# Fused preln layer: half of the first x loads, and the four writes of the second normalised rows, issued by ScalarE instead of SyncE

## The reference

```python
def ternary_quantize(w):
    delta = 0.7 * jnp.mean(jnp.abs(w))
    return jnp.where(w > delta, 1.0, jnp.where(w < -delta, -1.0, 0.0))

x = x + dynconv(_layernorm(x), w_lin)     # softmax taps, 31 wide, causal, 16 heads of 64
x = x + einsum("bsd,od->bso", _layernorm(x), ternary_quantize(weight) * alpha) + bias
```

## Time and profile before

| | us |
|---|---|
| runs shown | 418.83 and 427.5, median 423.17 |
| profiled execution | 418.44 |
| its span, on core 4, the slowest | 416.9 |
| spans of the eight cores | 404.3 to 416.9 |
| PE / DVE / ACT busy on core 4 | 161.0 / 132.6 / 71.0 |

### The profile page before, as it was taken

How to read it: one execution, slowest core, us unless ns; L and a number is a source line. 1 busy time by engine, 2 the same in 40 slices (tenths; PEclk the granted TensorE clock), 3 DMA queues, 4 the chain that set the end, 5 groups by cost and what they waited for, 6 DMA issues and landing times.

```text
span 416.9 us, 2975 instructions; the slowest of 8 cores (404.3 to 416.9 us)
## 1 busy us (share of the span) xinstructions
PE 161.0 (39%) x934; PEld 92.4 (22%) x940; DVE 132.6 (32%) x250; ACT 71.0 (17%) x78; POOL 5.8 (1%) x8
## 2 busy tenths in 40 slices
PE   0000030420300070016006769169430099999690
PEld 0000000100000030002002669169430033343230
DVE  1222592258220031103302297527360013232221
ACT  0000346751211023103201100000005341200000
POOL 5000000000000000000000000000000000000000
PEclk9999985855555577559556855555555579999896
DMA  7999824000499954974461599999403756999422
GB/s 179 288 300 282 283 108 100 0 1 0 101 179 224 253 101 102 234 141 99 150 158 25 119 199 241 222 182 232 74 0 112 108 142 149 259 274 241 128 101 101
DMA packets 85544, 64.53 MB, mean 155 GB/s; under 512 B 69008, under 2 KB 70032, under 8 KB 85528
## 3 DMA queue, kind: packets, MB, share of 16 engines
q10 hardware_dynamic: 13072, 37.82, 32.3%
q1 hardware_dynamic: 71352, 25.50, 31.3%
q0 software_dynamic: 1104, 1.02, 1.7%
HBM read 23.14 MB, written 25.40 MB: 116 GB/s over the span
## 4 chain that ended last, share of the span: by engine, by line
DMA 35%; SPq 27%; DVE 11%; PE 10%; ACT 7%; issue 4%; DVEq 3%; ACTq 2%
SPq L224 10%; DMA xs<-x 9%; SPq L207 9%; SPq L199 8%; DMA stage<-wpad 6%; DMA xn2d<-xn2r 6%; DMA xn1d<-xn 5%; DMA wet<-stage 4%; PE ps_at L617 3%; PE ps_wp L590 3%; DMA xn1T<-xn1d 3%; ACT wet L447 2%; ACT wet L446 2%; DVE redt L313 2%; DVE statsw L137 2%
## 5 line engine op out<-in xcount | busy, mean ns | idle before, releaser
L590 PE MATMUL ps_wp<-wlTb,xn1T 128*128 128x496 bf16 x128 | 37.4, 462 | 128.3 <-DMA xn1T<-xn1d 105.1
L617 PE MATMUL ps_at<-wins,wet 128*64 128x64 bf16 x512 | 50.8, 305 | 24.5 <-DMA wet<-stage 18.0
L617 PEld LDWEIGHTS ps_at<-wins,wet 128*64 128x64 bf16 x512 | 50.2, 216 | 25.4 <-issue 25.4
L590 PEld LDWEIGHTS ps_wp<-wlTb,xn1T 128*128 128x128 bf16 x128 | 14.3, 115 | 151.0 <-issue 142.8
L347 DVE TENSOR_REDUCE sumc<-wpad 128x16 f32<-128x496 bf16 x16 | 10.7, 669 | 110.7 <-ACT wpad L463 110.5
L642 PE MATMUL ps_ff<-wtern,xn2T 128*128 128x512 bf16 x64 | 26.7, 417 | 28.4 <-DMA xn2T<-xn2d 28.1
L137 DVE BATCH_NORM_STATS2 statsw<-xs 128x6 f32<-128x512 f32 x32 | 22.0, 688 | 31.4 <-DMA xs<-x 30.0
L554 ACT ACTIVATE xn2r<-xs,scn,scr 128x1024 bf16<-128x1024 f32 x16 | 18.5, 1228 | 52.9 <-DVEq L380 26.5
L357 DVE TENSOR_TENSOR xs<-ps_at,xs 128x1024 f32<-128x1024 f32 x16 | 19.6, 1223 | 23.7 <-PE ps_at L617 23.7
L640 PE MATMUL ps_ff<-wtern,xn2T 128*128 128x512 bf16 x60 | 25.1, 418 | 3.3 <-DMA xn2T<-xn2d 3.3
L463 ACT ACTIVATE wpad<-ps_wp,cstb 128x496 bf16<-128x496 f32 x16 | 10.6, 671 | 86.0 <-PE ps_wp L590 60.6
(11 more groups left out here) (83 smaller groups left out, 98.6 us busy)
## 6 DMA issues: line engine op xcount, KB each, us to landing
stage<-wpad ACTq DMA_DIRECT2D x16, 512.2 KB, 6.5
wins<-xn1d ACTq DMA_DIRECT2D x16, 512.0 KB, 10.9
out<-outst ACTq DMA_DIRECT2D x8, 1024.0 KB, 5.5
wTf<-wT ACTq DMA_DIRECT2D x1, 4096.0 KB, 32.9
xs<-x SPq DMA_DIRECT2D x4, 1024.0 KB, 28.4
xs<-x ACTq DMA_DIRECT2D x1, 4096.0 KB, 51.0
xn2d<-xn2r SPq DMA_DIRECT2D x4, 1024.0 KB, 5.1
xn1d<-xn ACTq DMA_DIRECT2D x3, 1024.0 KB, 4.8
```

Source lines behind the costliest of these rows:

```text
L590: mm = tensor.matmul(pw[:, 0:F], xn1T[:, cc * T + i * 128:cc * T + (i + 1) * 128], wlTb[:, cc * F:(cc + 1) * F], start=(cc == 0), stop=(cc ...
L617: mm = tensor.matmul(pa[64 * jj:64 * jj + 64, h * R:(h + 1) * R], lhsT, rhs, start=True, stop=True)
```

## The change

SP keeps the first and the third quarter of the first eight x tiles; the second and the fourth are issued by ACT, at the head of its program, ahead of `wTf`. In the feed-forward stage the four writes to `xn2_d` move from SP to ACT: after every fourth normalisation ACT drains and issues the write itself. SP keeps the wait for the write's landing and the transposing reads, and gets one new wait, once, for 24 of the convolution's 32 sub-tiles.

```diff
     @block.sync
         sync.dma_start(halox[:], halo_d[:]).then_inc(sems["ldh"], 16)
-        for q_ in range(4):
+        for q_ in (0, 2):
             sync.dma_start(
                 bass.AP(xs, 2 * q_ * C, [[NT * C, 128], [C, 2], [1, C]]),
...
         if level >= 5:
             for w in range(4):
-                sync.wait_ge(sems["xn2a"], 4 * (w + 1))
-                sync.dma_start(
-                    bass.AP(xn2_d, 4 * w * 128 * C, [[C, 128], [128 * C, 4], [1, C]]),
-                    bass.AP(xn2r, 0, [[4 * C, 128], [C, 4], [1, C]]),
-                ).then_inc(x2ws[w], 16)
+                if w == 0 and level >= 4:
+                    sync.wait_ge(sems["agg"], 24)
                 sync.wait_ge(x2ws[w], 16)
...
     @block.scalar
+        for q_ in (1, 3):
+            scalar.dma_start(
+                bass.AP(xs, 2 * q_ * C, [[NT * C, 128], [C, 2], [1, C]]),
+                bass.AP(x_d, 2 * q_ * 128 * C, [[C, 128], [128 * C, 2], [1, C]]),
+            ).then_inc(xqs[q_], 16)
         scalar.dma_start(
             bass.AP(wTf, 0, [[8 * C, 128], [C, 8], [1, C]]),
...
+                if i % 4 == 3:
+                    w_ = i // 4
+                    scalar.drain()
+                    scalar.dma_start(
+                        bass.AP(xn2_d, 4 * w_ * 128 * C, [[C, 128], [128 * C, 4], [1, C]]),
+                        bass.AP(xn2r, 0, [[4 * C, 128], [C, 4], [1, C]]),
+                    ).then_inc(x2ws[w_], 16)
```

## The result

| | before | after |
|---|---|---|
| median of all runs, us | 421.22 (10 runs) | 408.36 (11 runs) |
| ratio, with its 95% interval | | 0.9707 (0.9665 to 0.975) |
| profiled execution, us | 418.44 | 412.27 |
| its slowest core, span | core 4, 416.9 | core 2, 410.7 |

That is 2.9 per cent or 12.3 us less (0.0293 x 421), where 14.0 were forecast. The forecast of 404.4 started from 418.44; with the measured ratio that start gives 406.2. The median itself, 408.36, stands just past the forecast's own range of 400 to 408 and inside 399 to 413.

A forecast was written before the change was run, and what follows sets the result against it. A serial thread waiting for the last lower x quarter was taken to bound the start, TensorE nearly all of the feed-forward stage: 418.44 - 12.0 (loads) - 2.0 (writes) = 404.4 us, own range 400 to 408, wider range 399 to 413.

The forecast's parts named there:

- What bounds the start: Start: a serial thread hangs on the last lower x quarter at 42.8 us; later stages move as much, up to feed-forward.
- The sum for the start: Loads: by packet count the last quarter lands at 25.9, weights at 38.6 and 40.4, sums start 41.1; gain taken 12.0 us.
- That the gap behind the x data would turn into a wait for the weights: Start: both weights land after VectorE is ready, setting the gain at 12.0 us; with neither late, 14.5.
- 38 to 41: Sign of being right: the feed-forward weight's sums on VectorE (L313) start at 38 to 41 us.
- over 2: Sign of being wrong: PE's first feed-forward tile comes over 2 us later behind the first normalisation.
- GpSimd's own pace: Rival, loads: GpSimd's queue keeps its pace, projection weight stays at 44.3, gain 6.1, time 410.3; chance 0.14.
- The first loads gain nothing: Rival, loads: three queues share one rate, last lower quarter still lands near 42.8, time 416.4; chance 0.07.
- The second part: Feed-forward stage: writes moved from SP to ACT remove PE's later wait; gain 2.0 us, from -1.5 to 3.0.
- with hardly such a wait on core 3: Feed-forward tail: core 3 is only 1.2 us over the ideal, so the second part alone is worth 1.8.
- 1.0 for the second write on the first transposes: Feed-forward start: the second write beside the first transposes delays PE's start by 1.0 us, bounds 0 and 4.5.
- the fourth rival: Feed-forward: output DMAs starve behind ACT's writes, each us costing one from about 355; time 423 at 19 us late; chance 0.04.

The follow-up runs named there:

- e1: The change with its second part undone: only the loads changed, SP writes the second normalised rows as before; ratio to before 0.9711.
- e2: The change with its first part undone: only the four writes move to ScalarE, loads as before; ratio to before 0.997.
- e3: The change, but ScalarE issues all four lower x quarters and SP none; no ratio, median of six runs 414.69 us.
- r0: The change unaltered, measured again beside other kernels on the same chip; ratio to before 0.9695.
- r1: The change unaltered, measured a third time, as neighbour of e10; ratio to before 0.9784.
- e9: e8 but with SP writing the second normalised rows as before the change; ratio to before 0.9681.
- e8: e5 unaltered, measured again on another chip as neighbour of e9; ratio to before 0.9682.
- e5: The change, with the feed-forward weight in four DMAs and six of VectorE's eight sums ahead of the projection weight's square; ratio to before 0.9588.
- e10: e7 unaltered, measured again beside r1; ratio to before 0.9576.
- e4: The change, but GpSimd issues the projection weight before it clears its tile; ratio to before 0.9673.
- e7: The change with e3's load order, the feed-forward weight in four DMAs, and four sums on either side of the square; ratio to before 0.9592.

## Why the prediction was right

**What bounds the start: right.** The program hung on the last lower quarter of x, and the gain arrived in every later stage. First sign 11.0 us sooner on the mean, with e1 against e2 (55.1 and 66.3) 11.2.

**The sum for the start: right, and 1 us too large.** The packet count gave 38.6 for the projection weight, 40.4 for the feed-forward weight and 41.1 for the sums on core 4; measured were 39.2, 42.0 (2.10 + 39.9) and 42.1. Quarter 2 was there at 24.6 instead of 25.9. I then took 12.0 instead of the 11.7 that the count gave, and core 4's sums moved by 52.78 - 42.09 = 10.7. So from the last quarter to the two weights it took 14.6 and 17.4 us, where the count had 12.7 and 14.5. Two reasons show in the queues of core 4. The count let SP's queue end with its last quarter, but smaller transfers stood behind it: 95 more packets between 24.6 and 39.2 us. And a round of two queues, taken from shares of a round of three as 0.0196 us, is 0.021 from 28 to 33 us (243 and 236 packets). That the quarter came 1.3 us early hid part of it. That the gap behind the x data would turn into a wait for the weights was the step on which the size hung: without it 14.5 would have been the forecast.

Of the signs that were written down, the sums at 42.1 are 1 us past "38 to 41", and one sign of being wrong did come: the first feed-forward tile is 2.5 us later behind the first normalisation, where "over 2" was the limit. It belongs to the second part, below.

**GpSimd's own pace: refuted.** The projection weight landed at 36.9 to 39.2 on the eight cores and not at 44.3, the queues moved 415 and 416 packets, and in e3 the weight came 4.7 us sooner still with one queue fewer.

**The first loads gain nothing: refuted** as a whole. By the Trainium skill (DMA: Bandwidth & Descriptors, "Issuing engines are not separate DMA queues") issuing from several engines saves only issue time, and e3 agrees with it: one queue did as well as two, 53.6 against 53.8. What the rule doesn't speak of is what stands ahead of what, and that was worth the 11 us. The last lower quarter was there at 24.6, not near 42.8.

**The second part: mechanism right, two terms mis-sized.** The step "with hardly such a wait on core 3" held: only the slowest core counts, and the writes of 5.38 and 9.39 us that SP waited for in the chain were worth next to nothing. PE's wait and the slow clock behind it went, and the tail became 61.5 on all cores of the profile after. The term "1.0 for the second write on the first transposes" measured 2.4 (leads of 29.7 and 29.6 with the moved writes, 27.2 and 27.3 without). The other term is the one of the fourth rival, which the prediction lets cost from 355 us on. That bound took the output DMA's landing as it was before, about 5.8 us, and asked only when it leaves. On core 0 of e2 it left at 358.87, 11.9 behind the first addition, where the bound stands 14.6 behind it (355 less 340.35): by that there was nothing to pay. It took 12.8 us to land behind the fourth write, and the tail grew by 7.0. So this rival takes part of the gain at a far lower point, and on some cores costs 3 to 9 us of tail: core 0 of e2, cores 6 and 7 of r0, core 7 of r1. Forecast 2.0; measured 1.3 (e2, 0.3 per cent of 428, between -0.2 and 2.7), 0.7 by e1 against r0 (0.9711 and 0.9695, far inside their intervals), and none by e9 against e8. The forecast of 2.0 was some 1 us too large, which these intervals can't tell from nothing.

Together: 11.0 and about 1 against the 12.3 measured. The forecast was 12.0 and 2.0.

## What to carry to other kernels

Where a serial thread waits for input and all queues are busy, count packets: what stands ahead in the same queue, and how many queues take turns. Moving the first-needed data ahead of the later-needed is worth the difference of the landings, less what the next input down the thread is then late; look up that second landing before you write down the first as the gain. And before a transfer is moved to another engine's program, see what already stands behind it there: here it was the output DMAs, and the share of the chain of waits that the move seemed to free was not the time that TensorE was short of. Whether output DMAs on another queue would keep the tail at 61.5 wasn't tried. The version with the weight in pieces (e5, and e10 with all lower x on one queue) gave 0.9588 and 0.9576 beside the change's 0.9695 and 0.9784 on the chip where they were neighbours; only the second pair's intervals are apart.

## What the runs showed of the hardware that was not expected

Turns are counted in packets, not in bytes, and also between a hardware and a software queue: 415 against 416 packets in 8.9 us, but 1.70 MB against 0.41. A transfer in packets of 1 KB thus takes as many turns as one four times its size in packets of 4 KB: GpSimd's queue moved 1104 packets for 1.02 MB in the first 60 us of core 4 after, where 4 MB of x are 1024.

A write of 1 MB beside eight transposing reads delays the last of those by about 2 us (11.9 us from first issue to last landing become 13.9), and the first feed-forward addition by 2.4. The write itself takes anything from 4.2 to 5.1 us, the first of each core, ahead of all transposes, to 10.2, the fourth of e2's core 0; and a DMA of 1 MB right behind such a write in the same queue took up to 13.0 (e4 and e7, core 0), where 5.1 to 6.7 were usual before. What makes a write slow on one core and not on its neighbours is open; it wasn't tried.
